# Fetching the first layer's output weights behind the feed-forward product, in a two-layer cross-attention kernel

## The reference, cut to what matters

```
# layer 0
q = rmsnorm(x) @ wq; k = ctx @ wk; v = ctx @ wv          # 16 heads of 64
x = x + softmax(q k^T) v @ wo                            # wo: 1024 x 256
# layer 1, 16 heads of 16
x = x + causal_mha(ln1(x)) @ m_proj_w + m_proj_b
x = x + cross_mha(ln2(x), ctx) @ c_proj_w + c_proj_b
x = x + relu(ln3(x) @ f_w1 + f_b1) @ f_w2 + f_b2         # f_w2: 1024 x 256
```

## Time and profile before

| | |
|---|---|
| median of 3 runs | 5192.05 us (5190.23 to 5194.09) |
| the profiled execution's own time | 5187.58 us |
| its span, first to last instruction | 5185.8 us |
| PE busy | 4998.9 us, 96% |
| ACT busy | 4157.3 us, 80% |
| DVE busy | 3033.2 us, 58% |
| POOL busy | 698.7 us, 13% |
| one turn of the loop | 78.7 us |
| granted TensorE clock, mean | 0.990 |

### The profile page before, as it was taken

One profiled execution on the slowest core, in us unless ns is written; L12 is line 12 of the kernel. 1 busy time (PEld: TensorE's weight loads), 2 busy tenths in 40 slices (PEclk: granted clock), 3 DMA queues, 4 the chain that ended last, 5 costly groups with the idle time before them and its releaser, 6 DMA issues. The chain is left out here.

```text
span 5185.8 us, 148766 instructions
## 1 busy us (share of the span) xinstructions
PE 4998.9 (96%) x49240; PEld 4123.6 (80%) x49240; DVE 3033.2 (58%) x7921; ACT 4157.3 (80%) x17044; POOL 698.7 (13%) x1227
## 2 busy tenths in 40 slices
PE   6999999999999999999999999999999999999996
PEld 5788888888888888888888888888888888888885
DVE  4555655665665666556556556656655665565563
ACT  4788888888888888888888888888888888888884
POOL 0111111111111111111111111111111111111110
PEclk8999999999999999999999999999999999999997
DMA  3112112112112121121121121121221211211211
GB/s 111 61 56 79 62 56 78 60 58 78 46 73 78 42 76 65 55 76 62 56 79 62 56 78 59 60 78 45 74 78 42 76 63 56 77 62 56 79 58 37
DMA packets 101414, 337.76 MB, mean 65 GB/s; under 512 B 8720, under 2 KB 66896, under 8 KB 68048
## 3 DMA queue, kind: packets, MB, share of 16 engines
q0 software_dynamic: 36576, 266.35, 13.9%
q1 hardware_dynamic: 64496, 68.39, 4.0%
HBM read 313.74 MB, written 20.97 MB: 65 GB/s over the span
## 5 line engine op out<-in xcount | busy, mean ns | idle before, releaser
L606 ACT ACTIVATE ps<-ps,negmax 128x77 f32<-128x77 f32 (+2 forms) x6144 | 2063.4, 367 | 307.0 <-DVE negmax L823 305.3
L606 ACT ACTIVATION_READ_ACCUMULATOR ps<-ps,negmax 128x1 f32 x6144 | 1460.2, 244 | 0.8
L823 DVE TENSOR_REDUCE negmax<-ps 128x4 f32<-128x308 f32 (+2 forms) x1792 | 924.3, 563 | 222.1 <-PE ps L1094 90.6
L538 POOL TENSOR_TENSOR small<-small 128x1 f32<-128x1 f32 (+1 forms) x448 | 258.2, 576 | 2551.9 <-DVE small L800 2278.7
L995 PE MATMUL ps<-tail_h,coTh 128*128 128x256 f32 x2048 | 593.1, 290 | 3.4 <-DVE coTl L923 2.8
L818 DVE TENSOR_TENSOR zTl<-ps,zTh 128x256 fp32r<-128x256 f32 x512 | 210.6, 422 | 624.7 <-ACT zTh L586 624.5
L996 PE MATMUL ps<-tail_l,coTh 128*128 128x256 f32 x2048 | 572.0, 279 | 0.0
L997 PE MATMUL ps<-tail_h,coTl 128*128 128x256 f32 x2048 | 571.7, 279 | 0.0
L680 ACT ACTIVATE probs<-ps 128x512 f32<-128x512 f32 x768 | 399.6, 620 | 130.9 <-PE ps L1165 130.9
L995 PEld LDWEIGHTS ps<-tail_h,coTh 128*128 128x128 f32 x2048 | 385.3, 188 | 42.5 <-issue 34.9
L996 PEld LDWEIGHTS ps<-tail_l,coTh 128*128 128x128 f32 x2048 | 386.0, 188 | 0.0
(11 more groups left out here) (207 smaller groups left out, 12288.9 us busy)
## 6 DMA issues: line engine op xcount, KB each, us to landing
tail_h<-parted_f POOLq DMA_DIRECT2D x64, 1024.0 KB, 5.1
tail_l<-parted_f POOLq DMA_DIRECT2D x64, 1024.0 KB, 7.0
tail_h<-parted_wo POOLq DMA_DIRECT2D x63, 1024.0 KB, 5.2
tail_l<-parted_wo POOLq DMA_DIRECT2D x63, 1024.0 KB, 7.1
xin<-x_dram SPq DMA_DIRECT2D x64, 256.0 KB, 3.3
x<-x_dram SPq DMA_DIRECT2D x64, 256.0 KB, 2.7
out<-xr SPq DMA_DIRECT2D x64, 256.0 KB, 2.2
cin<-ctx_dram SPq DMA_DIRECT2D x64, 77.0 KB
```

The lines of the kernel that those rows point to most:

```text
L538: nc.gpsimd.tensor_tensor(rstd[:, stage, ts], veps[:, stage, ts], minus_half[:, ts], ALU.pow).then_inc(rstd_ready[stage], 1)
L606: ins = nc.scalar.activation(scores, scores, ACT.Exp, bias=negmax[w][:, t, h:h + 1], accum_out=sums[w][:, t, h:h + 1])
L823: nc.vector.tensor_reduce(dst, bank(s)[:, 0:heads * width].rearrange("p (h k) -> p h k", h=heads), AX_X, ALU.max, negate=True).then_inc(ma ...
```

## The change

The fetch of `wo` is issued by GpSimd directly behind its wait for the second `f2`, as the last thing of a turn, in place of behind the sum of `norm.2.1` of the next turn. The same two transfers of the same size are issued, as often as before.

```
@@ in run() of GpSimd, step "norm" @@
                         nc.gpsimd.tensor_tensor(xr[:, t, :], xs[:, t, :], row[:, k - 1, :], ALU.add).then_inc(xr_ready, 1)
-                        if step == ("norm", 2, 1) and ("wo", 0) in order:
-                            load_parts("wo")
@@ in run() of GpSimd, behind the second "wo" or "f2" @@
                         if isinstance(b, int):
                             pool.wait_ge(parts_out, 64)
-                        if later and not (later[0] == "wo" and ("norm", 2, 1) in c.after):
+                        if later:
                             load_parts(later[0])
```

## The result

The changed kernel takes 5247.57 us (4 runs, 5244.52 to 5248.08), the kernel before 5191.98 (4 runs): ratio 1.0107, 95% interval 1.0091 to 1.0123. It is 56 us slower, an interval clear of 1, where no change was forecast. In the profiles of the changed kernel, lines behind 559 have numbers lower by 2 than before.

The account below looks back on a forecast made before the run. PE, busy 96% of the span, was taken to bound the kernel. 62 fetches x 0 plus at most 1.2 us once counted as 0, so the median stays at 5192 us; range 5184 to 5205.

Parts of the forecast that it names:

- the duration of the store: Store of y issued by SP beside the moved fetch: 2.2 us now, taken as 6.3 us, at no cost.
- the row of the same case: Trace of the kernel before, once behind the loop: store issued 0.18 us behind a fetch takes 5.7 us.
- The upper bound: Store of y in the loop lands no earlier than the fetch beside it, at 2524.73: 7.9 us.
- The chain: From late store through POOL's sum of norm.2.0, root of stat.2.1 and VectorE's z of tile 1 to TensorE's turns; cost 0.
- The store may take 7.7 us: Longest store of y that costs nothing, counted back from z of tile 1 on VectorE at 2525.86.
- The first rival: Store lands with the fetch and PE waits: 43 us at the most, priced at 25 us slower, 5217 us; 9%.
- this clash for z of tile 0: VectorE's z beside GpSimd's sum: 0.64 us becomes 0.41, or up to 0.2 longer; taken as 0, not reaching PE.
- POOL's root of rms not late: POOL's queue behind f2: two issues take 1.22 us of idle time, 1.3 us is left over; cost 0.
- VectorE's statistics not held up by the issues: VectorE's statistics at 2517.30 beside GpSimd's fetch issues: taken as 0, with 0.1 us per turn kept above.
- the second rival: Fetch issues hold up VectorE's statistics 0.1 to 0.3 us per turn: 6 to 19 us slower, middle 5204; 5%.
- An earlier fetch gains nothing: Fetch of wo already lands 3.2 us before the first product that reads it; landing some 9.5 us earlier gains 0.
- the third rival: Fetch leaves a crowded stretch, ending PE's 0.27 us wait for ScalarE: at most 17 us faster, 5175; 7%.

Follow-up runs that it names:

- the sums late: Changed kernel, with GpSimd's two sums of norm.2 and its wait for the store moved behind the root of stat.2.1: 5194.52 us, 1.0008 of the kernel before.

## Why the prediction was wrong

**The step that failed** is the duration of the store: "I take 6.3, nearer to the row of the same case, as the difference is only 0.2 us of lead". It measured 8.4. The 0.2 us were not a small part of a slope but the whole of a step: the runs with a fetch 0.26 and 0.11 us ahead gave 8.2 and 3.1 us. The one row of 5.7 us lay on the step, and a value read off there says nothing about the place 0.2 us beside it. The 0.2 us should have been turned into packets: in the row about half of the store was through before the fetch's first packet, in the loop none of it.

**The upper bound failed too**, by 0.5 us. It was called the landing of the fetch "beside it", with the fetch's 7.7 us from the row behind the loop. But there half the store was already gone; where both run together to the end, the fetch takes 8.0 us and the store's landing comes 0.2 us behind the fetch's: 2546.17 + 8.4 = 2554.57 against 2546.35 + 8.0 = 2554.35. What the prediction drew from the skill's rule, that the store would end together with the fetch, came true; the sum went by the row instead.

**The chain held, and its threshold as far as it was tried.** "The store may take 7.7 us" agrees with the runs as far as they reach: 5.8 us cost nothing to speak of, 8.2 and 8.4 us did cost; nothing between was measured. It may lie a little lower, since the threshold leaves out that a late z of tile 1 also takes longer (below). The late store reached PE in exactly the links named, and taking one of them away (the sums late) took the loss away with the store still at 8.3 us.

**The first rival was right in its mechanism and too small.** It was given 9% and 25 us, 43 at the most; that most was worked out for a store of 8.4 us, which is what came, and 56 us were measured. 8.4 - 7.7 is 0.7 us per turn, and the turn grew by 1.0. The rest lies in z of tile 1, which takes 0.80 us where 0.41 was counted: once late, it meets GpSimd's second sum, which follows the root at once. The prediction had weighed this clash for z of tile 0 alone, and there it went as said (0.40 us, worth nothing). The Trainium skill has it in "SBUF — State Buffer", section "🔬 SBUF: two separate sides": the pair of ports that VectorE and GpSimd share is held for a whole instruction. The trace agrees: beside a sum z takes 0.64 and 0.80 us and ends 0.15 us behind the sum's end both times, and away from it 0.40 us.

**The rest, point by point.** The fetch starts 0.14 us behind `passed`: right. POOL's root of rms not late: right, 1.37 us of idling left of 2.44. VectorE's statistics not held up by the issues: right, 0.75 us as before, so the second rival falls. (The row that this was read from was weak: of the statistics at 2543.45 only 0.16 us lie beside an issue.) An earlier fetch gains nothing, and the old place cost nothing: right, since with the fetch behind the root of rms the time is 1.0003 of before; so the third rival falls too. What followed from the store of 6.3 us came out otherwise with it: POOL's wait of 0.3 to 1 us is 2.85, the root of stat.2.1 and z of tile 1 are not at their old places, and the turn isn't 78.7 us.

## What to carry to other kernels

Before a large prefetch is moved, look for the small transfers of other queues that will be in flight beside it, and for who waits for them in order: a store of 256 KB went from 2.2 to 8.4 us, and it hurt because a root was queued behind the wait for it. A duration taken from one overlapping pair holds for that order of arrival; with 0.15 us of difference it can be another, so the range must then take both ends. Three cures brought the time back to within 0.1% of the kernel before: issue the prefetch behind the store (3 us later), move the wait behind what is urgent on its engine, or make the prefetch of packets as small as the store's, which here let the store go first. And look at the packets before a run is taken as proof of a mechanism: the small packets gave the expected time for another reason.

## What the runs showed of the hardware

- The step. A store of 256 KB (256 packets of 1 KB) takes 2.2 us alone or 0.34 us ahead of a 2 MB fetch of 8 KB packets by GpSimd, 3.1 us (median) at 0.11 us behind the fetch's issue, 8.2 us at 0.26 and 8.4 us at 0.41 us. Behind the loop, 0.19 us behind, two stores took 5.8 and 7.1 us.
- Turns by packets. Where the two run together, as many packets of the store start as of the fetch, 92 and 90 in 2 us, at 0.09 and 0.73 MB.
- Small rows begin later. GpSimd's fetch of `f`, with no store near, has its first packet 1.64 us behind its issue in rows of 1 KB, 1.29 us in rows of 8 KB (medians of 61 turns).
- The place of tiles in SBUF. Two unused tiles that shift all later ones by 16 bytes per partition made the kernel 1.0025 (1.0014 to 1.0036) times as long; the group of 128x256 matmuls shown above reads 281 ns on average in place of 279. Why was not tried.
